# Row maxima of two softmax layers: turned by VectorE and written by DMA into spare query rows, instead of turned by TensorE and added in PSUM

## The reference, cut to what matters

```python
scores = einsum('bthd,bshd->bhts', q, k) * scale
attn = softmax(scores, axis=-1)      # exp(scores - max over keys), divided by its sum
out = einsum('bhts,bshd->bthd', attn, v)
```

## Time and profile before

| | value |
|---|---|
| median of three runs | 2077.3 us |
| the profiled execution, own time | 2076.24 us |
| its span, first to last instruction | 2074.4 us |
| PE, DVE, ACT, POOL busy in the span | 94%, 76%, 67%, 10% |
| mean granted TensorE clock | 0.981 of full speed |
| first pass of a0 (L1069) | 512 instructions, 586.9 us busy on DVE |
| first pass of a1 (L1069) | 256 instructions, 294.7 us busy on DVE |
| softmax stage of a0, about | 25 to 657 us of the span |
| softmax stage of a1, about | 734 to 1069 us of the span |

### The profile page before, as it was taken

How to read it: one execution, slowest core, us unless ns; L and a number is a source line. 1 busy time by engine, 2 the same in 40 slices (tenths; PEclk the granted TensorE clock), 3 DMA queues, 4 the chain that set the end, 5 groups by cost and what they waited for, 6 DMA issues and landing times. The chain is left out here.

```text
span 2074.4 us, 43441 instructions
## 1 busy us (share of the span) xinstructions
PE 1955.2 (94%) x17202; PEld 858.4 (41%) x17202; DVE 1574.4 (76%) x2254; ACT 1386.3 (67%) x2761; POOL 208.4 (10%) x388
## 2 busy tenths in 40 slices
PE   8999999999999979999998999999999899999998
PEld 4222222222223422222233666666665344444453
DVE  7999999999995599999946667776774655555553
ACT  4899999999998549899875666666774422222253
POOL 3011111110111330111100000000000200000000
PEclk7999999999999979999999999999999999999999
DMA  3000010110101020101010011110111055555510
GB/s 102 2 24 20 23 31 16 31 25 14 32 11 28 1 57 12 30 19 41 8 29 6 13 26 26 26 26 16 23 23 39 14 128 121 122 122 120 120 45 21
DMA packets 76041, 82.63 MB, mean 40 GB/s; under 512 B 23744, under 2 KB 58560, under 8 KB 71888
## 3 DMA queue, kind: packets, MB, share of 16 engines
q1 hardware_dynamic: 74896, 79.06, 16.0%
q0 software_dynamic: 528, 0.43, 0.1%
q10 hardware_dynamic: 432, 0.56, 0.1%
HBM read 62.98 MB, written 2.42 MB: 32 GB/s over the span
## 5 line engine op out<-in xcount | busy, mean ns | idle before, releaser
L1069 DVE TENSOR_REDUCE a0nm<-ps 128x2 f32<-128x1024 f32 x512 | 586.9, 1215 | 11.0 <-PE ps L936 8.8
L1047 ACT ACTIVATE a0p<-ps 128x512 f32<-128x512 f32 x1024 | 544.1, 599 | 60.4 <-PE ps L956 43.6
L970 PE MATMUL ps<-a0p,a0vst 128*32 128x256 f32 x4096 | 328.0, 392 | 27.4 <-ACT a0p L1047 14.0
L1069 DVE TENSOR_REDUCE a1nm<-ps 128x2 f32<-128x1024 f32 x256 | 294.7, 1217 | 7.2 <-PE ps L936 6.3
L1047 ACT ACTIVATE a1p<-ps 128x512 f32<-128x512 f32 x512 | 275.6, 596 | 34.4 <-PE ps L956 25.5
L956 PE MATMUL ps<-a0qm,a0k 32*128 32x512 bf16 x1024 | 277.3, 387 | 0.0
L2157 ACT ACTIVATE ex_s<-ps 128x512 f32<-128x512 f32 x128 | 76.4, 597 | 253.0 <-PE ps L2112 253.0
L936 PE MATMUL ps<-a0k,a0q 32*128 32x512 bf16 x1024 | 203.5, 395 | 17.9 <-DVE a0nm L1069 15.7
L2246 DVE TENSOR_TENSOR ex_su<-ex_s,ps 128x512 f32<-128x512 f32 x128 | 88.0, 688 | 114.2 <-PE ps L2116 113.7
L1757 PE MATMUL ps<-cak,caq 64*128 64x512 f32 (+3 forms) x768 | 171.3, 521 | 2.1 <-DVE canm L1909 2.1
L970 PE MATMUL ps<-a1p,a1vst 128*32 128x256 f32 x2048 | 164.1, 393 | 6.4 <-ACT a1p L1047 5.5
(11 more groups left out here) (327 smaller groups left out, 2495.0 us busy)
## 6 DMA issues: line engine op xcount, KB each, us to landing
ex_wb<-ex_w_dram SPq DMA_DIRECT2D x62, 512.0 KB, 6.2
xc_res<-car_dram SPq DMA_DIRECT2D x32, 256.0 KB, 4.2
xc_res<-a0rec SPq DMA_DIRECT2D x15, 256.0 KB
a0q<-a0parts_sb SPq DMA_DIRECT2D x95, 32.0 KB, 2.0
a1q<-a1parts_sb SPq DMA_DIRECT2D x94, 32.0 KB
a0k<-a0parts_sb SPq DMA_DIRECT2D x90, 32.0 KB, 2.0
a1k<-a1parts_sb SPq DMA_DIRECT2D x84, 32.0 KB
f2wg<-in_ex_gate SPq DMA_DIRECT2D x32, 64.0 KB, 1.8
```

Of the source, the lines that this page charges most:

```text
L970: last = pe.matmul(R.ps[32 * j:32 * j + 32, 6, cols], vst[:, g, s, j * HG // 4, :], p[:, s % 2, j, cols], start=(g == 0 and s == 0 and hal ...
L1047: act.activation(p[:, s % 2, e, :], R.ps[:, score_bank(n), :], ACT.Exp).then_inc(exp_done, 1)
L1069: dve.tensor_reduce(nm[:, u % 2, tb, 2 - 2 * z:4 - 2 * z, hf], R.ps[:, bank:bank + 2, :], X_AXIS, ALU.max, negate=True).then_inc(bank_free, 1)
```

## The change

DVE keeps the maxima in another order, joins them by a two-operand minimum, and turns the split parts itself, as 32 by 32 blocks (`dve.transpose` of 128x64 bf16). POOL then issues eight DMAs a unit, each of 32 runs of 64 bytes, which put the turned parts into spare rows of the queries `q` in place. `score` reads `q`; `qm`, PE's transposes and `merge` are gone. POOL's split has four instructions instead of five. Since slots of `q` are used again, the loads of queries of groups 4 and up also zero the spare rows, by one more DMA on SP. The first pass runs nine slots ahead instead of six (LEAD); `join` moves to the end of step 3, the turn to the end of step 4. A unit starts on PE when the eight DMAs have landed.

```diff
+def load_queries(A, idx, slot, queue):
+    load_rows(A, idx, slot, 0, queue)
+    if idx >= 4:
+        queue.dma_start(A.q[A.spare_rows, slot, :, :], A.zero_rows[:]).then_inc(A.ld[slot], 16)
...
+    LEAD = 9
-    qm = sb("qm", [128, 2, RT, CW], BF16)
-    mt = sb("mt", [128, 4, 4, ROWS], BF16)
+    mt = sb("mt", [128, 4, 4, 4], BF16)
+    mr = sb("mr", [128, 2, 2, 32], BF16)
...
-        return i // 4, i // 2 % 2, i % 2
+        return i // 4, i // 2 % 2, (i + LEAD) % 2
...
-        slots = [(u + 1 + n // 16, n % 16) for n in (6 + 2 * s, 7 + 2 * s)]
+        slots = [(u + 1 + n // 16, n % 16) for n in (LEAD + 2 * s, LEAD + 1 + 2 * s)]
...
         def split(u):
+            part, none, done = mt[:].rearrange("p h k t -> p k h t"), zero[:, 0:4, 0:4], 4 + u * 3
+            pool.wait_ge(mt_step, 3 * u + 1)
+            pool.tensor_tensor(part[:, 0], m0[:], none, ALU.add).then_inc(pool_step, 1)
+            pool.wait_ge(pool_step, done + 1)
+            pool.tensor_tensor(m1[:], m0[:], part[:, 0], ALU.subtract).then_inc(pool_step, 1)
+            pool.tensor_tensor(part[:, 1], m0[:], part[:, 0], ALU.subtract).then_inc(pool_step, 1)
+            pool.wait_ge(pool_step, done + 3)
+            pool.tensor_tensor(part[:, 2], m1[:], part[:, 1], ALU.subtract).then_inc(mt_step, 1)
+        def maxima_rows(u):
+            _k, chunk_i, _g, slot = place(u)
+            pool.wait_ge(mt_step, 3 * u + 3)
+            for i in range(4):
+                for pair in range(2):
+                    rows = slice(7 + 64 * pair, 64 + 64 * pair, 8) if RT == 1 else A.spare_rows
+                    to = q[rows, slot, pair % RT, chunk_i * CW:chunk_i * CW + CW].rearrange("p (t i r) -> p t i r", t=4, i=4)
+                    pool.dma_start(to[:, :, i, :], mr[32 * i:32 * i + 32, u % 2, pair, :]).then_inc(rows_in, 16)
...
             split(u + 1)
+            maxima_rows(u + 1)
             if u and u % 2 == 0:
                 divide(u // 2 - 1)
...
-                      qm[rows, u % 2, rt, :], start=True, stop=True).then_inc(p2_full, 1)
+                      q[rows, place(u)[3], rt, place(u)[1] * CW:(place(u)[1] + 1) * CW], start=True, stop=True).then_inc(p2_full, 1)
...
-            pe.wait_ge(bank_free, emptied("turn", u))
+            pe.wait_ge(rows_in, 128 * (u + 1))
...
         def join(u):
             dve.wait_ge(bank_free, emptied("max", u, 15))
-            dve.tensor_reduce(m0[:], nm[:, u % 2], X_AXIS, ALU.min).then_inc(max_ready, 1)
+            dve.tensor_tensor(m0[:], nm[:, u % 2, :, :, 0], nm[:, u % 2, :, :, 1], ALU.min).then_inc(mt_step, 1)
+        def turn(u):
+            dve.wait_ge(mt_step, 3 * u + 2)
+            if u >= 2:
+                dve.wait_ge(rows_in, 128 * (u - 1))
+            dve.transpose(mr[:, u % 2].rearrange("p a r -> p (a r)"), mt[:].rearrange("p h k t -> p (h k t)")).then_inc(mt_step, 1)
```

More of the change, by code:

```diff
@@ L159, in __init__ @@
         self.heads_of_group, self.mask = heads_of_group, mask
-        self.spare = (7, 15, 23)
+        self.spare_step = rows // 4
+        self.spare_rows = slice(7, 128, self.spare_step)
         self.scale = dim ** -0.5
@@ L166, in __init__ @@
         self.n_pool_loads = 4 * self.row_tiles
+        self.zero_rows = None
         self.inited = [nc.alloc_semaphore(name + "inited0"), nc.alloc_semaphore(name + "inited1")]
@@ L437, in load_mask @@
              .then_inc(A.ld[slot], 16)
+def load_queries(A, idx, slot, queue):
+    load_rows(A, idx, slot, 0, queue)
+    if idx >= 4:
+        queue.dma_start(A.q[A.spare_rows, slot, :, :], A.zero_rows[:]).then_inc(A.ld[slot], 16)
 def load_group(A, idx, slot, queue):
-    load_rows(A, idx, slot, 0, queue)
+    load_queries(A, idx, slot, queue)
     load_rows(A, idx, slot, 1, queue)
@@ L776, in slot_of @@
     def slot_of(i):
-        return i // 4, i // 2 % 2, i % 2
+        return i // 4, i // 2 % 2, (i + LEAD) % 2
     def ahead(u, s):
-        slots = [(u + 1 + n // 16, n % 16) for n in (6 + 2 * s, 7 + 2 * s)]
+        slots = [(u + 1 + n // 16, n % 16) for n in (LEAD + 2 * s, LEAD + 1 + 2 * s)]
         return [x if x[0] < UNITS else None for x in slots]
     def turns_at(u, s):
[L787 to L794, removed]
+        return s == 4 and u + 1 < UNITS
+    turns = [("max", u, i) for u in range(UNITS) for i in range(16)]
     turns += [("spread",)]
@@ L847, in on_sp @@
                 load_group(A, 2 * kk, kk % 2 * 2, sp)
[L848 removed]
+                load_queries(A, 2 * kk + 1, kk % 2 * 2 + 1, sp)
             if n >= 2 and not c and kk - 1 < PAIRS:
@@ L865, in on_pool @@
         pool.memset(zero[:], 0.0).then_inc(pool_step, 1)
-        pool.wait_ge(pool_step, 3)
+        pool.memset(A.zero_rows[:], 0.0).then_inc(pool_step, 1)
+        pool.wait_ge(pool_step, 4)
         def stage_v(g):
@@ L901, in on_pool @@
         split(0)
+        maxima_rows(0)
         stage_v(1)
@@ L928, in p1_slot @@
                 by_pool = 0 if slot else A.n_pool_loads
-                pe.wait_ge(ld[slot], 16 * ((kk // 2 + 1) * A.n_loads - by_pool))
+                pe.wait_ge(ld[slot], 16 * ((kk // 2 + 1) * A.n_loads + kk // 2 - by_pool))
                 if u == 0:
@@ L937, in p1_slot @@
                           k[rows, slot, rt, hf * CW:(hf + 1) * CW], start=True, stop=True).then_inc(bank_full, 1)
[L939 to L948, removed]
         def score(u, s, e):
@@ L987, in on_pe @@
                 A.among_maxima[i]()
[L988 to L991, removed]
+        for i in range(LEAD):
             p1_slot(1, i)
@@ L1012, in on_pe @@
                     pv(*before, 1)
-                if turns_at(u, s):
-                    turn(u + 1)
         def last_products():
@@ L1068, in reduce @@
             bank = dve_bank("max", u, i)
-            dve.tensor_reduce(nm[:, u % 2, tb, 2 - 2 * z:4 - 2 * z, hf], R.ps[:, bank:bank + 2, :],
+            dve.tensor_reduce(nm[:, u % 2, 2 - 2 * z:4 - 2 * z, tb, hf], R.ps[:, bank:bank + 2, :],
                               X_AXIS, ALU.max, negate=True).then_inc(bank_free, 1)
@@ L1096, in on_dve @@
             reduce(0, i)
+        reduce(1, 0)
         join(0)
-        for i in range(4):
+        for i in range(1, 3):
             reduce(1, i)
-        merge(0)
-        for i in range(4, 6):
+        turn(0)
+        for i in range(3, LEAD):
             reduce(1, i)
@@ L1107, in on_dve @@
                     reduce(*slots[0])
-                if s == 5 and u < UNITS - 1:
-                    join(u + 1)
                 if slots[1]:
                     reduce(*slots[1])
+                if s == 3 and u + 1 < UNITS:
+                    join(u + 1)
                 if turns_at(u, s):
-                    merge(u + 1)
+                    turn(u + 1)
         if A.maps:
```

25 lines of the change are left out of this document (3 added, 22 removed).

## The result

The changed kernel takes 2099.95 us (median of 4 runs, 2098.03 to 2100.79) against 2077.46 us before: a ratio of 1.0111, 95% interval 1.0099 to 1.0124. It is slower by 22 us where I had forecast 9 us less. The profiled execution took 2100.24 us, 24.0 more than the one of before, so its trace holds the whole difference.

What follows compares the result with a forecast made beforehand. DVE was taken to set the pace of both stages, with PE close behind in a1. The terms -17.5 - 2.1 + 6.4 + 2.3 + 2.0 = -8.9 us against 2076.24 gave a forecast of 2068 us, range 2056 to 2105.

Steps and rivals of the forecast that it cites:

- The turn on DVE: DVE's chain of maxima: a 0.22 us transpose replaces a 0.60 us turn, 46 x 0.38 = 17.5 us saved.
- PE without transposes: Units of a1: DVE no longer waits for a late PE after a turn, 14 x 0.15 = 2.1 us saved.
- a smaller loss behind `take`: Even units of a1: the 0.64 us lost behind `take` might shrink to a0's 0.23, 3 us more saved.
- Rival D: PE becomes the bound of a1, leaving half of a1's gain: 2072 us, chance 0.07.
- The longer lead: Behind each layer's last maximum: ACT has six more exponentials to do, 3.2 us a layer, 6.4 us lost.
- Late keys of a1: Key loads for groups 5 and 7 of a1 come 1.0 us late in each place, 2.0 us lost.
- The issues: POOL's eight DMAs a unit: wake-up 0.08, pitch 0.52, landing 2.3, rows in 6.0 us after the transpose's end.
- Rivals A and C: POOL's issues: A, 0.73 us pitch, 2121 us, chance 0.20; C, each waits for a DVE maximum, 2296 us, chance 0.03.
- The even units: Units where the rows' flight meets the reciprocals' 256 KB spread: rows 0.1 us late, 23 x 0.1 = 2.3 us lost.
- a margin of 0.2 to 0.3: At a unit's start: rows in at 6.0 us after the transpose; PE may start up to 6.3 (a1 6.2) without loss.
- Rival B: Only even units are late, by 0.5 us, behind the reciprocals' 256 KB and key loads: 2077 us, chance 0.22.
- My own upper bound for these units: Even units: a landing of 3.1 us would make the rows 0.6 us late in each.

Runs made afterwards that it cites:

- e6: The changed kernel with a lead of eleven and the logarithm and reciprocal at step 3 in place of 5; 2059.35 us, ratio 0.9917.
- e3: The kernel before with the longer lead alone: nine slots ahead, join after step 3, turn after step 4; 2081.66 us, ratio 1.0025.
- e4: The changed kernel with eleven slots ahead instead of nine, join after step 2, turn after step 3; 2066.48 us, ratio 0.9953.
- e1: The changed kernel with ACT's logarithm and reciprocal in step 3 of an even unit instead of step 5; 2082.48 us, ratio 1.0025.
- e2: The changed kernel with the reciprocals' spread cut to eight rows, 16 KB instead of 256 KB (wrong results); 2077.31 us, ratio 1.0005.
- e13: The changed kernel with 130 idle waits on TensorE ahead of the layers and nothing else changed; 2094.31 us, ratio 1.0087.
- e9: e1 with sixty idle waits on TensorE ahead of the layers; 2078.08 us, ratio 1.0003.
- e10: e1 with thirty idle waits on TensorE ahead of the layers; 2081.81 us, ratio 1.0032.
- e12: e1 with 130 idle waits on TensorE ahead of the layers; 2067.25 us, ratio 0.9959.
- e11: The changed kernel with four extra unread matmuls ahead of TensorE's wait for the rows of odd units from the third; 2094.29 us, ratio 1.0090.
- e8: The changed kernel with the reciprocals' spread and the loads queued behind it held on SP until the rows land; 2082.56 us, ratio 1.0035.

## Why the prediction was wrong

**The turn on DVE** (-17.5) and **PE without transposes** (-2.1) were right in kind and too small. The transpose takes 0.23 (I had 0.22), and nothing waits at it; but I had set its length against the 0.60 from the start of `merge` to the next maximum. From start to start the turn now takes 0.16 (164.53 to 164.69), so 0.44 goes each time and not 0.38. With rows on time the chains are 16.6 and 11.9 us shorter (e6 against before), 28.5 in all where I had 19.6. Of the surplus, 46 x 0.06 = 2.8 is that turn, 3.1 the `take` that no longer holds DVE up in a0 (e3); the rest, some 3 us, lies in a1, where I had left a smaller loss behind `take` as a bound. Rival D is out by the same figures: with rows on time a1 gains 11.9.

**The longer lead** (+6.4): 3.2 and 2.8 us in after, 6.0, as worked out.

**Late keys of a1** (+2.0): none at lead nine (e3, and none in after). They appear at eleven (e4).

**The issues**: pitch 0.54 (0.52), wake-up 0.30 (0.08), landing 1.6 (2.3), so PE starts 5.7 us after the transpose's end where the rows meet no other traffic (6.0 foretold), in time. Rivals A and C are out. By the Trainium skill (SBUF — State Buffer, Who interferes with whom) `tensor_reduce` on trn2 never locks GpSimd out; the trace agrees, with a pitch of 0.54 beside maxima without a gap. A landing of 1.6 for runs of 64 bytes, near the 1.4 of the row with 128, shows no sign that writes this short lengthen it; no run here varies their length.

**The even units, "0.1 late: 23 x 0.1 = 2.3 us lost"**, is the step that failed. But for the first of each layer they lose 0.7 to 3.8 us each. Against e6 the chains of after are 33.5 + 12.0 = 45.5 us longer, and the even units have some 40 of that; the unit at 361.55 (3.9) and small gaps in the others make up the rest. -28.5 + 45.5 + 6.0 = 23.0 of the 24.1 us between the spans; the rest is 0.8 at the start and small differences behind. Three things stand in place of the 0.1. With a margin of 0.2 to 0.3, my 0.1 late lets 256 KB and six loads on the same engines delay the rows by 0.3 to 0.4 only; e1 and e2 show that they cost far more, and in e13, where the packets have ended by 5.0 after the transpose, most by 4.3, PE still waits 1.6 to 2.2 us in most of a0's late units. I read no instruction traffic at all; e9, e10 and e12 show that a packet of it in the flight of the rows costs up to 2 us. And I had PE resume at full speed; the clock it came back with costs some 10 us more, by the estimate at e11. Rival B had the mechanism, and at 0.5 us it was priced at a quarter of what it cost. My own upper bound for these units, 0.6 us, came from a landing of 3.1; in after landings go up to 4.3.

The Trainium skill (DMA: Bandwidth & Descriptors) says that each DMA engine takes turns between its queues a packet at a time (Queues, rings and completion order), and that a transfer counts as landed only when its share on every engine is (Why a DMA increments its semaphore by 16 and not by 1). By these rules one engine held for 1.2 us by 16 KB would delay every transfer that has a share behind it, though 15 engines idle; e8's rows agree (landing 1.6 against 2.5), but which engine carried the packet the trace doesn't show.

**The unit at 350 us** (361.55 in after, 346 at lead eleven) stays open. In every kernel with row DMAs those of this unit start 3.1 us later than in all others, which costs 3.9 to 5.7 us with lead nine and 0.8 with lead eleven. GpSimd's timeline of after:

```profile
365.18 4.31 POOL L899 DMA_DIRECT2D a0q<-a0mr  x8 [4.74 <-issue]
```

With lead nine a packet of 8 KB on the second instruction queue (q14) starts 0.1 to 0.4 us after that transpose. But it does so in other units without harm, and with lead eleven it starts 2.5 us after it while the delay stays 3.1, so a refill of GpSimd's program is only a guess of mine, and a weak one.

## What to carry to other kernels

A DMA that a tuned engine waits for within a microsecond of its landing must be priced with everything that can fly beside it, and the bound for that is not the nearest landing in the trace: here the rows came 1.1 to 1.9 us after the other transfer's packet had ended. Buy slack before gain: two more slots of lead and an earlier reciprocal cost 4.5 us behind the last maxima and turned +22 us into -18. And when lateness comes and goes with no change in the work, look at the queues of kind instruction in the same window.

## What the runs showed of the hardware

- Waits that do nothing, at the start of TensorE's program, moved the time by 14 to 15 us (e1 to e12). With them moved the packets on the queue of kind instruction: 16 KB, 0.9 to 1.6 us each, one to some 262 matmuls and weight loads. Sixty waits moved the first ones 1.4 us.
- One such packet that starts 4.2 to 5.7 us after the transpose, while the last of eight small transfers are under way, made their consumer late in 50 of 50 units.
- After an idle stretch of 2.06 us the granted clock of TensorE was 0.50 for some 6 us, though it had work all the time; after another of 2.46 us it stayed 1.00. Waiting can cost twice.
- GpSimd's issue of a small DMA (2 KB, 32 runs of 64 bytes) takes 0.54 us, undisturbed by a VectorE that makes maxima without a gap, and lands in 1.6 us where it meets no other traffic; in after the longest landing was 4.3.
